# A masked attention with LayerNorm: the LayerNorm's steps spread over twelve slots, the first minimum of a block taken from two SBUF groups, and VectorE's subtractions issued a slot earlier

## What is computed

```python
scores = jnp.einsum('nd,md->nm', x, ks)
scores = jax.nn.leaky_relu(scores, negative_slope=0.2)
scores = jnp.where(adj > 0, scores, -9e15)
attn = jax.nn.softmax(scores, axis=1)
return layernorm(x + jnp.einsum('nm,md->nd', attn, ks))   # eps 1e-5
```

## The kernel before

| delay | engine and step | line |
| --- | --- | --- |
| 0 | PE `score`: 12 fp16 matmuls into one of two PSUM buffers; needs the mask of group g-2 done | L591 |
| 0 | ACT `bend`: leaky ReLU in PSUM, scaled down | L379 |
| 0 | DVE `mask`: adjacency minus scores into `ring` (SBUF, 24 groups) | L507 |
| 1 | DVE `least`: running minimum over groups, in PSUM | L523 |
| 19 | DVE `gap` and POOL `gap`: subtract the row's floor from 1 or 2 tiles (DVE) and 3 or 2 (POOL) of the group | L535, L295 |
| 21 | ACT `exponentials` | L383 |
| 22 | ACT `high_part`, then POOL `low_part`: the fp16 parts of two of the four tiles | L390, L305 |
| 23 | PE `weigh`: 4 fp32 matmuls (8 in the trace) and 12 fp16 into `weighted`; needs both parts | L626 |

## Time and profile before

### The profile page before, as it was taken

The page is one execution under the profiler, slowest core; times in us unless marked ns, Lnnn a source line. Parts: engine busy times, 40 slices in busy tenths (PEclk is TensorE's granted clock), DMA queues, the critical chain, the costliest instruction groups (busy, mean ns, idle before and its releaser), DMA issues.

```text
span 1669.5 us, 42465 instructions
## 1 busy us (share of the span) xinstructions
PE 1541.3 (92%) x16576; PEld 1429.8 (86%) x16576; DVE 1485.9 (89%) x1788; ACT 1466.5 (88%) x1842; POOL 1440.7 (86%) x1237
## 2 busy tenths in 40 slices
PE   2699999999999999999999999999999999999987
PEld 1499889889889889889889889889889889889887
DVE  6999889999889999889999889999889999889983
ACT  4599888989888989888989888989888989888986
POOL 1699889989889989889989889989889989889987
PEclk9999999999999999999999999999999999999999
DMA  9754445555445545445545445445455455445520
GB/s 357 269 196 175 170 170 187 177 179 179 170 172 184 177 180 177 172 170 185 177 180 179 169 172 186 177 177 184 166 173 186 177 177 182 167 174 186 176 77 7
DMA packets 67799, 296.33 MB, mean 177 GB/s; under 512 B 6160, under 2 KB 32784, under 8 KB 34832
## 3 DMA queue, kind: packets, MB, share of 16 engines
q1 hardware_dynamic: 67600, 293.63, 49.6%
HBM read 289.41 MB, written 4.19 MB: 176 GB/s over the span
## 4 chain that ended last, share of the span: by engine, by line
issue 37%; DVE 26%; POOL 26%; ACT 4%; PE 3%; DMA 2%; DVEq 1%; SPq 0%; POOLq 0%; ACTq 0%
DVE running L527 13%; POOL pt_lo L307 13%; POOL ring L303 11%; DVE ring L543 9%; DVE ring L518 3%; POOL rstd L321 1%; ACT pt_hi L393 1%; PE weighted L648 1%; DMA ring<-in_x_t 1%; ACT scores L381 1%; PE weighted L636 1%; DVE low L548 1%; ACT floor L404 1%; ACT ring L387 1%; DMA adj_sb<-in_adj 1%
## 5 line engine op out<-in xcount | busy, mean ns | idle before, releaser
L303 POOL TENSOR_TENSOR ring<-ring,floor 128x768 f32<-128x768 f32 (+2 forms) x512 | 779.2, 1522 | 49.8 <-ACT floor L404 49.8
L518 DVE SCALAR_TENSOR_TENSOR ring<-adj_sb,scores 128x1024 f32<-128x1024 int32 x512 | 623.1, 1217 | 118.4 <-ACT scores L381 116.5
L307 POOL TENSOR_TENSOR pt_lo<-ring,pt_hi 128x512 f16<-128x512 f32 x512 | 595.0, 1162 | 123.3 <-ACT pt_hi L393 123.2
L602 PE MATMUL scores<-xt_hi,kt_hi 128*128 128x256 f16 x2048 | 558.8, 273 | 80.9 <-DVE ring L518 51.2
L381 ACT ACTIVATE scores<-scores,shrink 128x1024 f32<-128x1024 f32 x512 | 551.2, 1077 | 60.5 <-PE scores L604 60.2
L527 DVE TENSOR_TENSOR running<-ring,running 128x1024 f32<-128x1024 f32 x480 | 586.8, 1223 | 0.1
L387 ACT ACTIVATE ring<-ring,lift 128x1024 f32<-128x1024 f32 x512 | 584.0, 1141 | 2.9 <-DVE ring L543 2.5
L604 PE MATMUL scores<-xt_hi,kt_lo 128*128 128x256 f16 x2048 | 559.2, 273 | 0.0
L603 PE MATMUL scores<-xt_lo,kt_hi 128*128 128x256 f16 x2048 | 558.8, 273 | 0.0
L636 PE MATMUL weighted<-k_rows,ring 128*128 128x129 f32 x4096 | 546.5, 276 | 2.3 <-DVE y L564 1.5
L636 PEld LDWEIGHTS weighted<-k_rows,ring 128*128 128x128 f32 x4096 | 499.4, 192 | 14.5 <-ACT ring L387 10.0
(11 more groups left out here) (54 smaller groups left out, 423.8 us busy)
## 6 DMA issues: line engine op xcount, KB each, us to landing
adj_sb<-in_adj SPq DMA_DIRECT2D x256, 1024.0 KB, 4.8
ring<-in_ks_t SPq DMA_DIRECT2D x8, 512.0 KB, 6.7
ring<-in_x_t SPq DMA_DIRECT2D x8, 512.0 KB, 12.9
xt_raw<-in_x_t SPq DMA_DIRECT2D x32, 128.0 KB, 4.8
x_row<-in_x SPq DMA_DIRECT2D x32, 128.0 KB, 4.9
out<-normed SPq DMA_DIRECT2D x32, 128.0 KB, 5.2
k_rows<-in_ks SPq DMA_DIRECT2D x16, 128.0 KB, 3.2
ring<-in_ks SPq DMA_DIRECT2D x1, 2048.0 KB, 9.2
```

The lines of the kernel that those rows point to most:

```text
L303: nc.gpsimd.tensor_tensor(here, here, below, ALU.subtract).then_inc(gap_ready, 1)
L307: nc.gpsimd.tensor_tensor(pt_lo[:, g % PARTS, :, :], ring[:, g % RING, WHOLE:, :], pt_hi[:, g % PARTS, :, :], ALU.subtract).then_inc(part_ ...
L518: nc.vector.scalar_tensor_tensor(ring[:, g % RING, :, :], adj_sb[:, n % ADJS, half * QUAD:(half + 1) * QUAD, :], 0.0, scores[:, g % 2, :, ...
L602: nc.tensor.matmul(to, kt_hi[:, cols], xt_hi[:, at, :], start=True, stop=False)
```

## The change

1. The LayerNorm's steps get other slots and places: `mean` stays at 7' (39) but goes ahead of POOL's `gap`; `squares_of` is cut into its two sides, at 8' and 10', each at the end of ACT's slot; `deviation` goes from 8' to 11', ahead of POOL's `gap`; `normalise` is cut in two, at 12' and 14', at the end of ACT's slot; `store` goes to slot 50.
2. The split of x for a block two blocks on moves earlier: `load_xt` from 8' to 2', ACT's `split_x` from 10' to 5', POOL's from 11', behind `gap`, to 6', ahead of it.
3. ACT's `first` goes away. DVE's `least` of group 1 takes the minimum of groups 0 and 1 straight from `ring`, and `running_ready` counts 15 a block.
4. DVE's `gap` is issued with delay 18 and not 19, except for a block's group 0, which stays at 19 (so slot 2' has none and slot 3' has two). In slot 0' `columns` goes ahead of `gap`; in the others `gap` still goes ahead of `least`.

```diff
--- before.py
+++ after.py
@@ -50,8 +50,12 @@
     AT_GAP, AT_EXP, AT_PART, AT_WEIGH = 19, 21, 22, 23
     LAST = GROUPS - 1
     AT_LOWEST, AT_TURN, AT_SPREAD = 17, 18, 19
-    AT_FIRST = 2
     AT_FINISH = LAST + AT_WEIGH
+
+    AT_MEAN, AT_DEVIATION, AT_STORE = AT_FINISH + 1, AT_FINISH + 5, AT_FINISH + 12
+    AT_SQUARES = (AT_FINISH + 2, AT_FINISH + 4)
+    AT_NORMALISE = (AT_FINISH + 6, AT_FINISH + 8)
+    AT_SPLIT_X = -11
     out_v = out.rearrange("(b j p) d -> b p j d", p=P, j=SIDES)
     x_v = x.rearrange("(b j p) d -> b p j d", p=P, j=SIDES)
@@ -175,7 +179,7 @@
             if count >= 1:
                 eng.wait_ge(semaphore, count)
-        SLOTS = range(ALL + AT_FINISH + 4)
+        SLOTS = range(ALL + AT_STORE)
         def group(slot, delay):
@@ -186,6 +190,11 @@
             b, over = divmod(slot - delay, GROUPS)
             return b if over == 0 and 0 <= b < BLOCKS else None
+
+        def least_count(g):
+
+            b, q = divmod(g, GROUPS)
+            return (GROUPS - 1) * b + max(q, 1)
         def dve_tiles(g):
@@ -229,12 +238,12 @@
             load_x(0)
             load_x(1)
             for s in SLOTS:
-                b = whole(s, AT_FINISH + 4)
+                b = whole(s, AT_STORE)
                 if b is not None:
                     store(b)
                 if s % LOAD == 1 and s // LOAD + ADJS < ALL // LOAD:
                     load_adj(s // LOAD + ADJS)
-                b = whole(s, -8)
+                b = whole(s, AT_SPLIT_X - 3)
                 if b is not None and b > 1:
                     load_xt(b)
                 b = whole(s, 20)
@@ -297,7 +306,7 @@
                 b = g // GROUPS
                 first = dve_tiles(g)
                 pool.wait_ge(floor_ready, b + 1)
-                pool.wait_ge(running_ready, g + 1)
+                pool.wait_ge(running_ready, least_count(g))
                 here = ring[:, g % RING, first:, :]
                 below = floor[:, b % 2, :].unsqueeze(1).to_broadcast([P, QUAD - first, BLOCK])
                 nc.gpsimd.tensor_tensor(here, here, below, ALU.subtract).then_inc(gap_ready, 1)
@@ -330,18 +339,18 @@
                 g = group(s, AT_PART)
                 if g is not None:
                     low_part(g)
-                g = group(s, AT_GAP)
-                if g is not None:
-                    gap(g)
-                b = whole(s, AT_FINISH + 1)
+                b = whole(s, AT_MEAN)
                 if b is not None:
                     mean(b)
-                b = whole(s, AT_FINISH + 2)
+                b = whole(s, AT_DEVIATION)
                 if b is not None:
                     deviation(b)
-                b = whole(s, -5)
+                b = whole(s, AT_SPLIT_X + 1)
                 if b is not None and b > 1:
                     split_x(b)
+                g = group(s, AT_GAP)
+                if g is not None:
+                    gap(g)
         @block.scalar
         def _(act):
@@ -404,33 +413,19 @@
                 nc.scalar.activation(floor[:, b % 2, :], floors[:, b % 2, :], ACT.Copy)\
                     .then_inc(floor_ready, 1)
-            def first(g):
-                act.wait_ge(masked_ready, g + 1)
-                wait(act, low_ready, g // GROUPS)
-                wait(act, running_ready, g)
-                nc.scalar.activation(running[:, :, :], ring[:, g % RING, :, :], ACT.Copy).then_inc(running_ready, 1)
-
-            def squares_of(b):
+            def squares_of(b, j):
                 act.wait_ge(mean_ready, b + 1)
-                for j in range(SIDES):
-                    wait(act, squares_ready, SIDES * b + j)
-                    nc.scalar.activation(squares[:, :], y[:, j, :], ACT.Square, bias=neg_mean[:, j:j + 1],
-                                         accum_out=square_sum[:, j:j + 1]).then_inc(squares_ready, 1)
-
-            def normalise(b):
+                wait(act, squares_ready, SIDES * b + j)
+                nc.scalar.activation(squares[:, :], y[:, j, :], ACT.Square, bias=neg_mean[:, j:j + 1],
+                                     accum_out=square_sum[:, j:j + 1]).then_inc(squares_ready, 1)
+
+            def normalise(b, j):
                 act.wait_ge(shift_ready, b + 1)
                 wait(act, out_stored[b % 2], 16 * (b // 2))
-                for j in range(SIDES):
-                    nc.scalar.activation(normed[:, b % 2, j, :], y[:, j, :], ACT.Identity, bias=shift[:, j:j + 1],
-                                         scale=rstd[:, j:j + 1]).then_inc(normed_ready, 1)
+                nc.scalar.activation(normed[:, b % 2, j, :], y[:, j, :], ACT.Identity, bias=shift[:, j:j + 1],
+                                     scale=rstd[:, j:j + 1]).then_inc(normed_ready, 1)
             for s in SLOTS:
-                b = whole(s, AT_FINISH + 2)
-                if b is not None:
-                    squares_of(b)
-                b = whole(s, AT_FINISH + 3)
-                if b is not None:
-                    normalise(b)
                 g = group(s, AT_PART)
                 if g is not None:
                     high_part(g)
@@ -445,12 +440,16 @@
                 b = whole(s, AT_SPREAD)
                 if b is not None:
                     spread(b)
-                b = whole(s, AT_FIRST)
-                if b is not None:
-                    first(b * GROUPS)
-                b = whole(s, -6)
+                b = whole(s, AT_SPLIT_X)
                 if b is not None and b > 1:
                     split_x(b)
+                for j in range(SIDES):
+                    b = whole(s, AT_SQUARES[j])
+                    if b is not None:
+                        squares_of(b, j)
+                    b = whole(s, AT_NORMALISE[j])
+                    if b is not None:
+                        normalise(b, j)
         @block.vector
         def _(dve):
@@ -523,11 +522,17 @@
             def least(g):
                 dve.wait_ge(masked_ready, g + 1)
                 here = ring[:, g % RING, :, :]
-                dve.wait_ge(running_ready, g)
-                nc.vector.tensor_tensor(running[:, :, :], here, running[:, :, :], ALU.min).then_inc(running_ready, 1)
+                if g % GROUPS == 1:
+                    dve.wait_ge(masked_ready, g)
+                    wait(dve, low_ready, g // GROUPS)
+                    so_far = ring[:, (g - 1) % RING, :, :]
+                else:
+                    dve.wait_ge(running_ready, least_count(g) - 1)
+                    so_far = running[:, :, :]
+                nc.vector.tensor_tensor(running[:, :, :], here, so_far, ALU.min).then_inc(running_ready, 1)
             def columns(b):
-                dve.wait_ge(running_ready, GROUPS * (b + 1))
+                dve.wait_ge(running_ready, (GROUPS - 1) * (b + 1))
                 wait(dve, turned_ready, b)
                 nc.vector.tensor_reduce(col_min[:, :], running[:, :, :].rearrange("p t n -> p n t"), AX.X, ALU.min)\
                     .then_inc(col_min_ready, 1)
@@ -537,7 +542,7 @@
                 b = g // GROUPS
                 tiles = dve_tiles(g)
                 dve.wait_ge(floor_ready, b + 1)
-                dve.wait_ge(running_ready, g + 1)
+                dve.wait_ge(running_ready, least_count(g))
                 here = ring[:, g % RING, 0:tiles, :]
                 below = floors[:, b % 2:b % 2 + 1, :].to_broadcast([P, tiles, BLOCK])
                 nc.vector.tensor_tensor(here, here, below, ALU.subtract).then_inc(dve_gap_ready, 1)
@@ -575,14 +580,17 @@
                 b = whole(s, AT_LOWEST)
                 if b is not None:
                     lowest(b)
-                g = group(s, AT_GAP)
-                if g is not None:
-                    gap(g)
                 g = group(s, 1)
-                if g is not None and g % GROUPS:
+                if g is not None and g % GROUPS == LAST:
                     least(g)
-                    if g % GROUPS == LAST:
-                        columns(g // GROUPS)
+                    columns(g // GROUPS)
+                for early in (False, True):
+                    g = group(s, AT_GAP - 1 if early else AT_GAP)
+                    if g is not None and early == (g % GROUPS > 0):
+                        gap(g)
+                g = group(s, 1)
+                if g is not None and 0 < g % GROUPS < LAST:
+                    least(g)
         @block.tensor
         def _(pe):
```

More of the change, by code:

```diff
@@ L332, in _ @@
                     low_part(g)
+                b = whole(s, AT_MEAN)
+                if b is not None:
+                    mean(b)
+                b = whole(s, AT_DEVIATION)
+                if b is not None:
+                    deviation(b)
+                b = whole(s, AT_SPLIT_X + 1)
+                if b is not None and b > 1:
+                    split_x(b)
                 g = group(s, AT_GAP)
@@ L335, in _ @@
                     gap(g)
-                b = whole(s, AT_FINISH + 1)
-                if b is not None:
-                    mean(b)
-                b = whole(s, AT_FINISH + 2)
```

(34 more changed lines are left out.)

## The result

The changed kernel takes **1580.72 us** (median of 4, 1580.53 to 1580.95) against 1673.8 for the kernel before in the same comparison: a ratio of 0.9445, interval 0.9428 to 0.9461. The prediction's 1591 (0.951) had the direction and 82 of the 93 us, but the lower end of its range was 1582 and does not hold the time.

What follows compares the result with a forecast made beforehand. PE was taken as the bound: 16 x 2.89 plus 3.82 us of holes a block. Saving 2.62 in each of 30 blocks (78.6) plus 3.5 in the tail gave 1591 us, own range 1583 to 1604, 8-in-10 range 1582 to 1620.

Steps and rivals of the forecast that it cites:

- four holes: PE's time over 2.89 us a slot: turn in 2' 0.75, spread in 3' 0.96, `finish` in 7' 0.25, slot 10' 1.86.
- LayerNorm (edit 1): Spreading its steps over slots makes ACT's and POOL's waits cost nothing, saving all 1.86 us of slot 10' a block.
- The split (edit 2): Moving the split of x earlier puts POOL's `gap` in 6' back by about 1.2 us, under cover: zero.
- `first` and `least` (edit 3): ACT is relieved of 1.7 us in 2' and 3'; PE doesn't wait there for ACT, so no gain or loss.
- the ping-pong: ACT and POOL waiting on each other in turn over LayerNorm steps, stopping PE in slot 10' for 1.86 us.
- The walk: Timing from the scores of 0': `least` of group 1 ends at 10.9, with 0.7 us free on DVE, so costs nothing.
- VectorE's order (edit 4): DVE's earlier `columns` and `gap` end PE's waits before turn and spread, saving 0.40 of 0.75 and 0.36 of 0.96.
- 0.27 and 0.52: Bounds in us for turn (2') and spread (3') with all lateness gone; block 47.28, time 1586.
- Only the ping-pong goes: Rival, 15%: DVE is still late at 0', turn and spread wait as now; 1614 us.
- The stall moves: Rival, 12%: the LayerNorm's stall moves to 11' to 13', POOL giving exponentials their differences late; 1.25 a block, 1629 us.
- Exclusion in 2': Rival, 5%: DVE's two-SBUF-input minimum and POOL exclude each other without cover, 1.4 us exposed; 1633 us.
- Slower: Rival, 3%: both engines' stalls add at `least` of group 1, 3.04 us with none hidden; 1682 us.

Runs made afterwards that it cites:

- e7: The kernel before with only DVE's new order of `gap`, `least` and `columns` added; 1677.44 us, ratio 1.0024.
- e6: The changed kernel with both the LayerNorm's steps and the split of x put back to their old slots; 1653.11 us, ratio 0.9876.
- e1: The changed kernel with only the LayerNorm's steps put back to their old slots and places; 1704.74 us, ratio 1.0191.
- e4: The kernel before with only the LayerNorm's new slots and places added; 1595.15 us, ratio 0.9535.
- e5: The changed kernel with only the split of x put back to its old slots; 1583.13 us, ratio 0.9461.
- e3: The changed kernel with ACT's `first` brought back and `least` no longer reading two SBUF tiles; 1582.8 us, ratio 0.9459.
- e2: The changed kernel with only DVE's old order put back, `gap` at delay 19 for all groups; 1593.87 us, ratio 0.9529.
- e8: The changed kernel with DVE's running minimum taken in pairs, so more instructions read two SBUF tiles; 1805.01 us, ratio 1.0782.

## Why the prediction was wrong

**What bounds the kernel** was right as to the places and sizes: 16 x 2.89 and four holes, and three of the four are what moved. "Nothing but PE could hold a block at 50 us" was wrong. The floor says what PE would take if nothing waited; it does not say that a hole is worth its length. e7 gave PE 0.84 and got nothing; e6 took 1.7 us off ACT besides and got 0.68 a block; and in e1 the same LayerNorm cost 3.13 and, with the clock, 0.83 more, where it cost 1.86 before.

**LayerNorm (edit 1)**: the waits cost nothing after it, as predicted; slot 10' is 2.89. Its share was too small in my account: 2.54 a block alone (e4), as the turn's wait also went with it.

**The split (edit 2)**: next to nothing in the changed kernel (0.07, e5), as predicted. But it only costs nothing because the mean no longer stands behind it with ACT waiting: in the company of the old LayerNorm it costs 1.10 a block of stall and 0.83 of clock (e1 less e6).

**`first` and `least` (edit 3)**: zero, as predicted, once the ping-pong is gone (e3); with the ping-pong in place it was worth 0.68 a block (e6 against e7), which the prediction did not see. The walk put DVE's two-input minimum at 9.8 to 10.9 after the scores of 0', beside POOL's `low_part` and ahead of its wait for the floor. That is where it is, and 0.31 is what it costs DVE, under 0.27 of DVE idle time that is still left.

**VectorE's order (edit 4)**: the step that failed is the pair of terms for turn and spread. The prediction said "For the saving I take 0.40 of 0.75" and "0.36 of 0.96", and held 0.27 and 0.52, read from a turn and a spread that had just waited, as the least they could cost. Measured: 0.53 of 0.75 and 0.52 of 0.96, leaving 0.22 and 0.44. Two things were off in the sizes. All of the lateness went (0.48 and 0.45) and not the larger part of it: 0.17 a block. And the work itself got shorter by 0.05 and 0.08, below the lower bound. e2 and e4 show that the second goes with the wait: in one trace each the turn, without a wait, costs 0.21 to 0.22, while the spread, 0.32 late, costs 0.84, that is 0.52 behind its start; without the wait it costs 0.44. A likely reason, argued and not tested, is that the weight load is no longer hidden behind a wait: the turn's begins 0.11 before its matmul in the changed kernel (827.02, 827.13), beside the last score matmul, and 0.01 before it in the kernel before (870.44, 870.45).

The cause was also put in the wrong place. The turn's whole 0.53 comes with edit 1 and without edit 4 (e4), so edit 4 gives 0.40 a block at the spread in place of the 0.76 taken for it, and edit 1 gives 2.54 and not 1.86. That the sum still came near is because all four edits went in together.

**The sum.** The 30 intervals from the second `columns` to the last gave 88.3 (117.94 to 1618.84 before, 118.41 to 1531.0 after) and not 78.6; the tail 3.2 and not 3.5; the start lost 0.5. 91.0 of span against 82.1, of which turn and spread are 30 x 0.29 = 8.7. The lower end of the range was built on bounds that were none: with 0.27 and 0.52 the sum gave 1586, and the range went 4 us below that; with 0.22 and 0.44 the same sum gives 1582.6 as its centre. The other 1.7 of the 10.6 us missed is the distance of the median from the profiled execution, which I carried over: it is 0.0 for the changed kernel (1580.71 and 1580.72).

**The rivals.** *Only the ping-pong goes*: out, and for a reason it hadn't, as the turn's wait went with the ping-pong. *The stall moves*: out, slots 11' to 13' at 2.89. *Exclusion in 2'*: the mechanism is there, its cover too; e8 shows it without cover: 0.85 more on the mean for each of seven such instructions, 5.9 us a block on DVE, of which the block shows 5.6 (with the pairing's own share), and 1.6 more where the clock falls. *Slower*: not here.

## What to carry to other kernels

Price a hole in the bounding engine's timeline only after asking what it is waiting for in turn: a stall that comes from two engines handing work back and forth within a slot can cause other waits several slots on, and can swallow what is gained elsewhere. An edit's worth depends on which of the others are in: measure it both alone and by taking it out. Give each handover a slot of distance, and put short steps that another engine needs ahead of the long one. A duration read from behind a wait is no lower bound of what the work costs without the wait; look for an instance that had none, or set the lower bound below it. A VectorE instruction with two SBUF inputs beside a busy GpSimd belongs where one of the two is idle anyway.

## What the hardware showed that I had not expected

- Two fp32 transposes cost PE 0.27 us behind a wait and 0.21 to 0.22 without one, four fp32 matmuls of 128 columns 0.52 and 0.44.
- A small GpSimd instruction pays the exclusion too: the mean's 0.19 us became 1.16 in e8.
- TensorE's granted clock fell from full speed (2.4 GHz) to 0.50 (1.2 GHz) for 3.4 us at a time in steady blocks of e1, e7 and e8 alone, each time behind PE's longest wait of the block, and a fall cost 0.8 to 1.7 us on top of the hole. The length of the hole does not decide it by itself. e1 has 3.13 over in 9' and 10' in every block and a fall in every other; e7 has 2.69 over in most blocks and no fall in 17 of them, and three of its seven falls come in blocks with only 2.16 over; e6, with 2.03, has none. What else decides is not shown.
- The same instruction with two SBUF inputs lasted 1.23 us with GpSimd idle (e1) and 2.87 behind two GpSimd instructions that followed one another without a gap (e5). The second left PE's slots 2' and 3' as they were.
